# A graph attention layer on one Trainium2 core: rows loaded as one run per partition, scores kept at both ends of a row

## The reference, cut to what matters

```python
K = typed_linear(x, Wk, bk, node_type)          # (6250, 192); Q and V in the same way
e0, e1, e2 = [cos(log(t + 1) * w_time + b_time) for t in edge_attr[:, 0:3].T]   # 32 values each
def edge_msgs(Kn, Qn, Vn, ek, eq):
    k = concatenate([Kn, ek], 1).reshape(-1, 4, 56)
    q = concatenate([Qn, eq], 1).reshape(-1, 4, 56)
    att = einsum('ehd,ed->eh', k, q.sum(1)) / sqrt(56)          # 4 scores an edge
    return att, concatenate([Vn, ek], 1).reshape(-1, 4, 56)
att, v = edge_msgs(K[row], Q[col], V[row], e1, e2)              # row = src, col = dst
att_i, v_i = edge_msgs(K[col], Q[row], V[col], e2, e1)
att, att_i = seg_softmax(att, col, n), seg_softmax(att_i, row, n)
agg = segment_sum([v * att, e0], col) + segment_sum([v_i * att_i, e0], row)     # 256 columns
o = typed_linear(concatenate([agg, agg], 1), Wa, ba, node_type)
# then two layer norms with residuals
```

## Time and profile before

| | us |
|---|---|
| median of three runs | 8411.55 (8407.98 to 8413.25) |
| span of the profiled execution | 8400.1 |
| exchange, first gather to last scatter | 2548.5 to 5527.4 |
| runs, softmax and weights of direction 0 | 5536.8 to 5782 |
| sum0, from its first row load to its end | 5782.2 to 7109 |
| of it the load of `crd`, first issue to end of the block | 6973.3 to 7109 |
| runs, softmax and weights of direction 1 | 7109 to 7259 |
| sum1 | 7259 to 8039 |

### The profile page before, as it was taken

How to read it: one execution, slowest core, us unless ns; L and a number is a source line. 1 busy time by engine, 2 the same in 40 slices (tenths; PEclk the granted TensorE clock), 3 DMA queues, 4 the chain that set the end, 5 groups by cost and what they waited for, 6 DMA issues and landing times. The chain is left out here.

```text
span 8400.1 us, 132655 instructions
## 1 busy us (share of the span) xinstructions
PE 5523.3 (66%) x34292; PEld 3955.2 (47%) x34293; DVE 6052.2 (72%) x8967; ACT 4416.4 (53%) x12537; POOL 5874.8 (70%) x6077
## 2 busy tenths in 40 slices
PE   7766666666666667667766677613777772499944
PEld 6456666666663333333333333312555552388833
DVE  8377777777777878878777888744666663788865
ACT  0144444444445666666666666513666662388833
POOL 3657777777777777777777777756777771288835
PEclk5877777777778888888888888866999996699967
DMA  2553344333437988989988988977999999599963
GB/s 76 182 179 110 108 120 118 108 113 108 124 88 254 296 293 294 292 296 295 293 293 291 296 293 295 263 224 256 392 389 388 389 387 112 153 287 288 289 202 87
DMA packets 1586579, 1957.54 MB, mean 233 GB/s; under 512 B 429865, under 2 KB 1388307, under 8 KB 1586075
## 3 DMA queue, kind: packets, MB, share of 16 engines
q1 hardware_dynamic: 1083870, 1023.67, 40.0%
q0 software_dynamic: 255392, 674.52, 25.2%
q10 hardware_dynamic: 247072, 257.15, 9.0%
HBM read 1100.44 MB, written 883.21 MB: 236 GB/s over the span
## 5 line engine op out<-in xcount | busy, mean ns | idle before, releaser
L1141 PE MATMUL exch_pG<-far_tab,exch_ohT 128*128 x3328 | 1630.4, 643 | 625.7 <-ACT exch_kc L1056 621.4
L1002 POOL DMA_INDIRECT exch_row<-table,exch_of x1664 | 1598.6, 961 | 547.8 <-issue 520.3
L888 POOL DMA_INDIRECT recs<-place_rec,place_addr x1568 | 1570.8, 1002 | 540.4 <-issue 506.6
L1604 PE MATMUL sum_pS<-sum_row,sum_oh 128*128 128x260 f32 x6656 | 1620.2, 403 | 362.7 <-DVE edge_acc L1654 327.5
L1604 PEld LDWEIGHTS sum_pS<-sum_row,sum_oh 128*128 128x128 f32 x6656 | 1292.7, 199 | 689.9 <-DVE edge_acc L1654 407.6
L1141 PEld LDWEIGHTS exch_pG<-far_tab,exch_ohT 128*128 128x128 f32 x3328 | 747.3, 231 | 1458.2 <-issue 1411.8
L1216 POOL DMA_INDIRECT bys<-sum_pb x920 | 895.0, 973 | 296.6 <-issue 271.7
L1622 ACT ACTIVATE sum_off<-kept_ramp,sum_neg 128x128 f32<-128x128 f32 x3120 | 953.5, 387 | 92.4 <-POOL sum_neg L1559 92.4
L1055 ACT ACTIVATE exch_pb<-exch_pG 128x192 f32<-128x192 f32 x1664 | 551.1, 331 | 466.8 <-PE exch_pG L1141 399.5
L1216 POOL DMA_INDIRECT bys<-exch_pb x624 | 642.7, 1030 | 204.5 <-issue 158.1
L716 PE MATMUL place_pA<-place_t_lo 128*128 128x128 f16 x3136 | 313.1, 260 | 626.8 <-ACT place_t_lo L673 623.6
(11 more groups left out here) (319 smaller groups left out, 11940.1 us busy)
## 6 DMA issues: line engine op xcount, KB each, us to landing
bys<-place_none SPq DMA_DIRECT2D x52, 4224.0 KB
spill<-exch_row SPq DMA_DIRECT2D x208, 1024.0 KB
sum_row<-bys SPq DMA_DIRECT2D x208, 1024.0 KB, 5.3
sum_row<-spill ACTq DMA_DIRECT2D x206, 1024.0 KB
mid<-exch_pb SPq DMA_DIRECT2D x208, 660.0 KB
sum_pb<-mid SPq DMA_DIRECT2D x184, 660.0 KB
exch_row<-table,exch_of POOLq DMA_INDIRECT x1664
recs<-place_rec,place_addr POOLq DMA_INDIRECT x1568
```

What stands on the lines that cost most here:

```text
L888: nc.gpsimd.indirect_dma_start(recs, bass.IndirectOffsetOnAxis(addr[:, par, t:t + 1], 0), rec[:, par, t, :], None).then_inc(s_scat[par], 16)
L1002: nc.gpsimd.indirect_dma_start(row[q][:, t, TD:TD + S.TW], None, table, bass.IndirectOffsetOnAxis(of[q][:, t:t + 1], 0)).then_inc(s_row[q] ...
L1141: nc.tensor.matmul(pG[t % 3][:, 0:GW], ohT[ring(j, 2)][:, t, :], flat[:, bass.ds(tiles[t] * GW, GW)], start=True, stop=True).then_inc(s_ga ...
L1604: last = nc.tensor.matmul(pS[j % SETS * HG + t // 2][:, 0:AW], oh[h][:, t, :], row[j][:, t, :], start=(t % 2 == 0), stop=(t % 2 == 1))
```

## The change

1. `spill` gets rows of 260 words instead of 256, so that a step's rows are one contiguous run of 8320 bytes in DRAM and in the tile `row` (the last four columns are overwritten by the weights). The load of sum0 takes the whole run. As the load now writes the columns of the weights, ACT copies the weights after it has waited for the load; the copy stands behind the one-hots (Relu) instead of ahead of them.
2. The order by source is laid out as `(p c)`: place s lies in row (s % 128) * 1664 + s // 128 of `bys`. A partition's rows are contiguous, and sum1 loads a step's rows as one run of 8704 bytes (tile `row` has 272 columns there, the values begin at column 5). DVE works the row number out of the place in the exchange with three more instructions on 128x8 words; padding records get the rank 2^25.
3. A row of `mid` and `bys` has RC = 272 words: scores and source (five words, PIECE) stand at its head and again at its tail; the values begin at 5, the place is at 265. DVE copies the scores to the head (a COPY of 128x8x4), ACT writes the source to both. The end of an even row and the head of the next odd one are 40 contiguous bytes with the scores of both, and the load of `crd` takes these: 128x104x10 words in eight DMAs where it was 128x208x5.
4. Small tiles of the exchange (`pick`, `place`, one of `at`) move into the tile `ones`, and `otile1` shares the tile of `otile0`.

```diff
-        self.SC = self.VW
-        self.SLOTC = self.SC + self.H + 1
+        self.PIECE = self.H + 1
+        self.VO = self.PIECE
+        self.WO = self.VO + self.VW
+        self.SLOTC = self.WO + self.H
+        self.RC = -(-(self.SLOTC + 1 + self.PIECE) // 8) * 8
+        self.SC = self.RC - self.PIECE
...
-                sp.dma_start(spill[:, bass.ds(n * G, G), :], row[q][:, :, 0:2 * TD + PROJ]).then_inc(s_v[q], 16)
+                sp.dma_start(spill[:, bass.ds(n * G, G), :], row[q][:, :, 0:S.VW + H]).then_inc(s_v[q], 16)
...
-                nc.scalar.activation(pb[r][:, :, S.SC + H:S.SC + H + 1], rec[q][:, :, S.SRC:S.SRC + 1], ACT.Copy)
+                nc.scalar.activation(pb[r][:, :, H:S.RC:S.SC], bc(rec[q][:, :, S.SRC], 2, 2), ACT.Copy)
...
-                nc.vector.tensor_tensor(pb[q][:, :, S.SLOTC].bitcast(I32), begin[:], mine[:, :, S.RANK], ALU.add)
+                link(nc.vector.tensor_tensor(place[:, 0], begin[:], mine[:, :, S.RANK], ALU.add))
+                nc.vector.tensor_scalar(place[:, 1], place[:, 0], P - 1, None, ALU.bitwise_and)
+                link(nc.vector.tensor_scalar(place[:, 2], place[:, 0], 7, None, ALU.logical_shift_right))
+                nc.vector.scalar_tensor_tensor(out=pb[q][:, :, S.SLOTC].bitcast(I32), in0=place[:, 1], scalar=float(NT), in1=place[:, 2],
+                                               op0=ALU.mult, op1=ALU.add)
...
-                nc.vector.tensor_reduce(pb[q][:, :, S.SC:S.SC + H], ck, op=ALU.add, axis=AX).then_inc(s_sco, 1)
+                link(nc.vector.tensor_reduce(pb[q][:, :, S.SC:S.SC + H], ck, op=ALU.add, axis=AX))
+                nc.vector.tensor_copy(pb[q][:, :, 0:H], pb[q][:, :, S.SC:S.SC + H]).then_inc(s_sco, 1)
...
-        eng.dma_start(row[j][:, :, 0:VW], rows_v[:, bass.ds(n * G, G), 0:VW]).then_inc(s_v[j], 16)
+        eng.dma_start(row[j][:], rows_v[:, bass.ds(n * G, G), :]).then_inc(s_v[j], 16)
...
-            v = bys.rearrange("(c p) f -> p c f", p=P)
+            v = bys.rearrange("(p c two) f -> p c (two f)", p=P, two=2)
+            pairs = crd[:].rearrange("p (c two) f -> p c (two f)", two=2)
...
-            for a in range(0, NT, NT // 8):
-                sp.dma_start(crd[:, a:a + NT // 8, :], v[:, a:a + NT // 8, S.SC:S.SC + H + 1]).then_inc(s_x, 16)
+            for a in range(0, NT // 2, NT // 16):
+                sp.dma_start(pairs[:, a:a + NT // 16, :], v[:, a:a + NT // 16, S.SC:S.SC + 2 * S.PIECE]).then_inc(s_x, 16)
...
-                nc.scalar.activation(row[j][:, :, VW:AW], al[:, bass.ds(n * G, G), :], ACT.Copy).then_inc(s_al, 1)
...
+            if bys is not None:
+                act.wait_ge(s_v[j], 16 * (i + 1))
             nc.scalar.activation(oh[h][:, 0:OT, :], x[:, 0:OT, :], ACT.Relu, bias=1.0, scale=-1.0).then_inc(s_oh, 1)
+            if bys is not None:
+                nc.scalar.activation(row[j][:, :, at0 + VW:at0 + AW], al[:, bass.ds(n * G, G), :], ACT.Copy).then_inc(s_al, 1)
```

More of the change, by code:

```diff
@@ L780, in _ @@
             dve.wait_ge(s_none, 1)
+            nc.vector.memset(none[:, S.H:S.H + 1], -1.0)
             nc.vector.memset(none[:, S.SC + S.H:S.SC + S.H + 1], -1.0).then_inc(s_none, 1)
@@ L931, in exchange @@
         rec = [s.sb(f"rec{n}", [P, G, REC]) for n in range(6)]
-        pick = s.sb("pick", [P, G, S.LN])
         begin = s.sb("begin", [P, G])
-        at = [s.sb(f"at{n}", [P, G, H + 1]) for n in range(2)]
+        spare, used = k.ones, G * S.LN + 3 * G
+        pick = spare[:, 0:G * S.LN].rearrange("p (t l) -> p t l", l=S.LN)
+        place = spare[:, G * S.LN:used].bitcast(I32).rearrange("p (a t) -> p a t", a=3)
+        at = [spare[:, used:used + G * (H + 1)].rearrange("p (t h) -> p t h", t=G), s.sb("at1", [P, G, H + 1])]
         of = [s.sb(f"of{n}", [P, G], I32) for n in range(R)]
@@ L1054, in gathered @@
                     act.wait_ge(s_gat, n * G + t + 1)
-                    nc.scalar.activation(pb[q][:, t, 0:PROJ], pG[t % 3][:, 0:PROJ], ACT.Copy)
+                    nc.scalar.activation(pb[q][:, t, S.VO:S.VO + PROJ], pG[t % 3][:, 0:PROJ], ACT.Copy)
                     nc.scalar.activation(kc[h][:, t, 0:DK + PROJ], pG[t % 3][:, PROJ:GW], ACT.Copy).then_inc(s_ev, 1)
@@ L1074, in cosines @@
                 act.wait_ge(s_fr[1], n + 1)
-                nc.scalar.activation(pb[q][:, :, PROJ:PROJ + 2 * TD], frac[:, :, 0:2 * TD], ACT.Sin, scale=-2 * math.pi)
+                nc.scalar.activation(pb[q][:, :, S.VO + PROJ:S.WO], frac[:, :, 0:2 * TD], ACT.Sin, scale=-2 * math.pi)
                 nc.scalar.activation(kc[h][:, :, DK + PROJ:DK + KE], frac[:, :, 0:TD], ACT.Sin, scale=-2 * math.pi)
@@ L1192, in step @@
                 mine = rec[ring(j, 6)]
-                link(nc.vector.tensor_tensor(pick[:], bc(mine[:, :, S.SET], 2, S.LN), bc(k.ramp[:, 0:S.LN], 1, G), ALU.is_equal))
-                link(nc.vector.tensor_tensor(pick[:], pick[:], row[q][:, :, RB:RQ], ALU.mult))
-                link(nc.vector.tensor_reduce(begin[:], pick[:], op=ALU.add, axis=AX))
-                nc.vector.tensor_tensor(pb[q][:, :, S.SLOTC].bitcast(I32), begin[:], mine[:, :, S.RANK], ALU.add)
+                link(nc.vector.tensor_tensor(pick, bc(mine[:, :, S.SET], 2, S.LN), bc(k.ramp[:, 0:S.LN], 1, G), ALU.is_equal))
+                link(nc.vector.tensor_tensor(pick, pick, row[q][:, :, RB:RQ], ALU.mult))
+                link(nc.vector.tensor_reduce(begin[:], pick, op=ALU.add, axis=AX))
+                link(nc.vector.tensor_tensor(place[:, 0], begin[:], mine[:, :, S.RANK], ALU.add))
[3 more added lines that the diff above has]
+                                               op0=ALU.mult, op1=ALU.add)
                 dve.wait_ge(s_ev, (n + 1) * G)
@@ L1512, in aggregate @@
     HG = G // 2
-    row = [s2.sb(f"row{n}", [P, G, AW]) for n in range(4)]
+    at0, wide = (0, AW) if bys is not None else (S.VO, S.RC)
+    row = [s2.sb(f"row{n}", [P, G, wide]) for n in range(4)]
     WT = G if bys is not None else G - 2
@@ L1559, in step @@
                 nc.gpsimd.tensor_copy(neg[j][:], k.less[:, bass.ds(n * G, G)]).then_inc(s_neg, 1)
-                nc.gpsimd.tensor_copy(row[j][:, :, VW:AW], al[:, bass.ds(n * G, G), :]).then_inc(s_al, 1)
+                nc.gpsimd.tensor_copy(row[j][:, :, at0 + VW:at0 + AW], al[:, bass.ds(n * G, G), :]).then_inc(s_al, 1)
                 pool.wait_ge(s_neg, n + 1)
@@ L1565, in step @@
                     nc.gpsimd.tensor_scalar(oh[j % 2][:, t, :], k.ramp[:], neg[j][:, t:t + 1], 0.0, ALU.add, ALU.is_equal)
-                r = row[j][:, WT:G, head:head + H * DK].rearrange("p t (h f) -> p t h f", h=H)
+                r = row[j][:, WT:G, at0 + head:at0 + head + H * DK].rearrange("p t (h f) -> p t h f", h=H)
                 nc.gpsimd.tensor_tensor(r, r, bc(al[:, bass.ds(n * G + WT, G - WT), :], 3, DK), ALU.mult).then_inc(s_wp, 1)
@@ L1603, in step @@
                     pe.wait_ge(s_add, n * HG + t // 2 + 1)
-                last = nc.tensor.matmul(pS[j % SETS * HG + t // 2][:, 0:AW], oh[h][:, t, :], row[j][:, t, :],
+                last = nc.tensor.matmul(pS[j % SETS * HG + t // 2][:, 0:AW], oh[h][:, t, :], row[j][:, t, at0:at0 + AW],
                                         start=(t % 2 == 0), stop=(t % 2 == 1))
@@ L1637, in weigh @@
             dve.wait_ge(s_v[j], 16 * (i + 1))
-            r = row[j][:, 0:WT, head:head + H * DK].rearrange("p t (h f) -> p t h f", h=H)
+            r = row[j][:, 0:WT, at0 + head:at0 + head + H * DK].rearrange("p t (h f) -> p t h f", h=H)
             if bys is not None:
@@ L1904, in gnn_resnorm @@
     recs = nc.dram_tensor("recs", [2 * P * S.NT, S.REC], F32, kind="Internal").ap()
-    spill = nc.dram_tensor("spill", [P, S.NT, S.VW], F32, kind="Internal").ap()
+    spill = nc.dram_tensor("spill", [P, S.NT, S.VW + S.H], F32, kind="Internal").ap()
     mid = nc.dram_tensor("mid", [P, S.NT, S.RC], F32, kind="Internal").ap()
@@ L1938, in gnn_resnorm @@
             k.head0 = S.TD
-            bys_v = bys.rearrange("(c p) f -> p c f", p=P)
+            bys_v = bys.rearrange("(p c) f -> p c f", p=P)
             with ExitStack() as ctx3:
```

14 lines of the change are left out of this document (7 added, 7 removed).

## The result

The changed kernel takes 8487.22 us (median of four, 8484.94 to 8488.36), the kernel before 8412.4 us beside it: a ratio of 1.009, with a 95% interval of 1.0078 to 1.0102. The forecast was 8352 us.

What follows compares the result with a forecast made beforehand. POOL was taken to bound the exchange and sum0, DMA packets the load of crd, PE sum1. Terms -64 - 3 + 4 + 2 + 1 = -60 us gave 8352 us; 8 in 10 range 8330 to 8405.

Steps and rivals of the forecast that it cites:

- The load of spill as one run: Sum0: longer runs need about 15% less DMA time, speeding the sum loop but not the stage; worth 0.
- rival C: Sum0: long spill runs crowd out POOL's scatters; 10% loss gives 8469 us; 8% for slower, 5% for an even result.
- The load of crd: After sum0: half as many packets, 40 bytes instead of 20, cut the load from 136 to 72 us; -64 us.
- Rivals A: Load of crd: the short packets cost more than half, gain only -32 us, 8380 us; chance 11%.
- B: Load of crd: packets cost less as a partition's scores lie close in DRAM; -78 us, 8334 us; chance 8%.
- E: Load of crd: bound by bytes, so the change does nothing; chance 1%.
- Divisions beside the scatters: End of sum0: DVE's divisions fall beside the last scatters, each then 1.50 us instead of 0.97; +4 us.
- DVE in the exchange: Exchange: 1.0 us more DVE work a step, covered by its waiting except two steps at the end; +2 us.
- DMA in the exchange: Exchange: about 1% more bytes raise the DMA share to 0.91, POOL remains the limit; worth 0.
- Rival D: Exchange reaches its DMA or DVE limit; 3 points of share beyond it give 8439 us; chance 4%.
- Sum1: Sum1: PE is the limit, so loading rows of bys by partition in 8704-byte runs is worth 0.
- The -3 for row loads out of the way: Start of the crd load: the sum loop ends earlier, removing row loads beside its first 4 us; about -3 us.

Runs made afterwards that it cites:

- e6_single: Changed kernel with spill loaded in two DMAs of 4160-byte runs and the crd scores fetched in 20-byte packets; 8410.96 us, timed once.
- e5_pitch264: Changed kernel with spill rows of 1056 bytes, a step's rows loaded by two DMAs of 4224-byte runs; 8341.65 us, ratio 0.9919 to the kernel before.
- e7_ring6: Changed kernel with six buffers instead of four in sum0's forwarding loop, 8320-byte runs kept; 8470.5 us, ratio 1.0074 to the kernel before.
- e10_start32: Changed kernel with spill rows stored and loaded in 1024-byte packets at a pitch of 1056 bytes; 8346.43 us, timed once.
- e11_paced1: Changed kernel, 8320-byte runs kept, with ACT making each step's one-hots twice to slow the sum loop; 8344.32 us, ratio 0.9930 to the kernel before.
- e1_short: Changed kernel with spill back at 256-word rows loaded as 1024-byte runs and ACT's weights copy ahead of the one-hots; 8351.41 us, ratio 0.9925.

## Why the prediction was wrong, point by point

**The step that failed** is the worth of 0 for "The load of spill as one run": "That makes the sum loop faster, not the stage: the scatters still take 920 x 1.278 us." The first half is right, and even the size: q10 moved 164.79 MB in 0.567 x 16 x 700 us of the engines' time, 25.9 bytes a ns, against 21.5 before. The second half isn't: they took 1315 us. I counted the cheaper rows as relief for the DMA engines, at an unchanged amount. But the loop was held back by exactly this resource, and here the loop took what was freed, and more: 235 GB/s at a share of 56.7%, where it had 181 at 52.8%. The sum that was not made needs only rows that I had: PE is busy for 71.7 of 100 us in sum0, with 278 matmuls, 16 a step, so 4.1 us a step; a loop with nothing to wait for would load 8320 x 128 bytes in that time, 260 GB/s. POOL's queues ask for 218 at the pace worked out under rival C, together 478, and no stretch shows more than 386.

**Rival C was what happened**, and at 8% for slower it was far too cheap. Its mark, POOL's gaps released by the load of `mid`, is the row shown above; its size was 12% instead of 10%. I let speak against it, in which q0 has its full pace beside long runs of q10. But that stretch has two queues, and the third was missing; a row that lacks the very thing in question is no evidence. The rule it was given, one packet in turn, is only roughly right. It gave 184, 120 and 96 GB/s, and 235, 93 and 90 came. The Trainium skill, "DMA: Bandwidth & Descriptors", section "Queues, rings and completion order", says that an engine goes round its queues, a packet of several descriptors at a time. The direction agrees with the runs at 8320 bytes, in which the queue with the longest runs got the most (235 of 418 GB/s) and the other two fell short. The amounts at 1 KB, where q10 moved the most bytes too, say that the turn isn't one run of each; what it is, no run here tells.

**The load of crd**: -64 forecast, -63.0 measured. The bound was the right one (the 32-byte row): 90646 packets in 60 us are 0.66 ns each. The queue from 7120 to 7180 is shown below. Rivals A, B and E fall, B by e6_single as well.

```profile
q1 hardware_dynamic: 90646, 3.62, 176.4%
```

**Divisions beside the scatters**: +4 forecast. They did fall beside scatters, and each scatter under them took 2.62 us and not the 1.50 of the earlier trace rows. In e5_pitch264:

```profile
6932.84 11.87 DVE L1692 TENSOR_TENSOR edge_acc<-edge_acc,sum_den 128x2744 f32<-128x2744 f32 x4
...
6934.16 2.62 POOL L1228 DMA_INDIRECT bys<-sum_pb  x1 [0.30 <-issue]
6937.08 2.62 POOL L1228 DMA_INDIRECT bys<-sum_pb  x1 [0.30 <-issue]
```

There are four of them, each 1.65 us longer: +6.6 us. The term was 2.6 us too small; the row that it was taken from was of another operation, on 1664 columns and not on 2744.

**DVE in the exchange**: 1.0 us a step forecast; (2305.2 - 2164.6) / 190 steps of 14.2 us are 0.74. That is busy time alone; with the three short waits that the forecast held as well, some 0.09 each by its own figure, it is about 1.0. The cover did hold it. DVE's wait for ACT shrank from 465.4 us to

```profile
DVE exch_frac L1182 <- ACT exch_frac L1055: 265.9, 164, 7.1
```

and POOL issued 2114 instructions in these 2700 us, where it was 2102. The last scatter starts at 5530.6 instead of 5526.5, +4.1 where +2 was forecast, and the wait there doubled. But e7_ring6, with the same exchange, has it at 5518.0, so one profile can't settle a term of 2 us.

**DMA in the exchange**: 0.91 forecast from the bytes, 1.00 measured. The mechanism was missing from the sum. The estimate by the Trainium skill, "DMA: Bandwidth & Descriptors", section "How a descriptor splits into AXI transactions", counted rows that don't start on a 256-byte boundary; it gave 0.94 and the right direction. But rows at a pitch of 1056 bytes miss that boundary nearly as often (seven in eight, against fifteen in sixteen at 1040), and the share is 0.90 there (e5_pitch264, e10_start32). The measurement decides: here 32 bytes matter and 256 don't. Rival D, the exchange at its DMA limit, came to the share that it names, and yet not to its price: POOL kept its pace at 1.00. A share of 1.00 isn't the limit, as the 1.05 of sum0 says.

**Sum1**: from its first to its last accumulation 758.7 us after, 757.1 before. 0 was right.

**The sum without the failed step** holds. e11_paced1 has every term of the changed kernel and POOL at its full pace: -60 us forecast, and 58.2 us faster than the kernel before on its chip (8344.3 against 8402.6). The -3 for row loads out of the way isn't seen: e6_single, whose loop ends before the load, needs 135.8 us for the old packets, and the kernel before 136.2. In e1_short the agreement is in part luck. The terms left there, -64 + 2 + 1, are -61 us, and it was 64 us faster (8351.4 against 8415.7); but its load of `crd` gained 46 us, not 63, and in its profile another 12 us come from an earlier first scatter (5783.0 against 5795.0), which nothing in the sum accounts for.

## What to carry to other kernels

When an edit makes a transfer cheaper for a loop that waits for it, write down what every queue will ask for at the loop's new pace, and compare the sum with what the engines have been seen to move: a loop off the critical path that becomes faster can take the DMA engines from the one on it. If the sum doesn't fit, keep the short-run form, cut the runs in two, or slow the loop on purpose to where it just finishes in time; each of the three gave 0.7 to 0.8% here, where the plain edit lost 0.9%. And where scattered words are loaded, count packets, not bytes (shown here for 20 to 40 bytes).

## What the runs showed of the hardware that I had not expected

- With full engines and three queues that ask for more than is moved, who gives way changed with the length of a run. Beside packets of about 5 KB and 4 KB on the other queues, a queue with runs of 1 KB or of 4 KB (two DMAs a step) yields; one with 8 KB runs takes 235 of 418 GB/s and the others get 84 to 87% of what they move at POOL's full pace.
- 20, 32 and 40 bytes cost 0.64, 0.67 and 0.66 ns a packet over all engines: no measurable difference.
- Rows of a store to DRAM that start on odd multiples of 16 bytes raise the share of all queues together from 0.90 to between 0.98 and 1.00, at nearly the same bytes; multiples of 32 bytes don't. The pitches tried were 1024, 1040 and 1056 bytes.
- Beside a division of DVE on whole tiles, POOL's issue of a scatter takes 2.62 us instead of 0.97.
- Four DMAs issued in a row by ACT took 1.9 to 2.2 us, two 0.85 to 0.89, and one with a single run for each partition 0.34. One with eight runs for each partition took 0.38 to 2.51 us in the kernel before (median 0.69).
